# Six edits around the expert blocks and the wide attention of a two-layer decoder kernel: a third PSUM bank, paired transposes, early activation tables, earlier block loads, later roots

## The reference, cut to what matters

```
x = _layernorm(x + _L0_attn_ref(x, ...))          # 16 heads of 8, rope, causal
x = _layernorm(x + _L0_xattn_ref(x, ctx_1024, ..., mask, ...))
x = _layernorm(x + _L0_ffn_ref(x, gate_w, wg, wu, wd))
x = _layernorm(x + _L1_attn_ref(x, W_qkv, W_out)) # 16 heads of 64
x = _layernorm(x + _L1_xattn_ref(x, ctx_1024, ..., mask, ...))
x = _layernorm(x + _L1_ffn_ref(x, W_fc, ln_w, ln_b, W_proj))

# _L0_ffn_ref: 8 experts, 2 per token
top_v, top_i = jax.lax.top_k(x_flat @ gate_w.T, 2)
probs = softmax(top_v)
hidden = jax.nn.silu(x_flat @ wge.T) * (x_flat @ wue.T)
acc + we[:, None] * (hidden @ wde.T)
```

## Time and profile before

| | us |
|---|---|
| median of 3 runs | 412.69 |
| lowest and highest of them | 410.81, 412.75 |
| the profiled execution, its own time | 409.98 |
| its span, first to last instruction | 408.0 |
| PE busy in the span | 347.2 (85%) |
| DVE busy | 252.6 (62%) |
| POOL busy | 186.3 (46%) |
| ACT busy | 183.7 (45%) |

### The profile page before, as it was taken

How to read it: one execution, slowest core, us unless ns; L and a number is a source line. 1 busy time by engine, 2 the same in 40 slices (tenths; PEclk the granted TensorE clock), 3 DMA queues, 4 the chain that set the end, 5 groups by cost and what they waited for, 6 DMA issues and landing times.

```text
span 408.0 us, 9801 instructions
## 1 busy us (share of the span) xinstructions
PE 347.2 (85%) x3718; PEld 263.3 (65%) x3718; DVE 252.6 (62%) x592; ACT 183.7 (45%) x386; POOL 186.3 (46%) x267
## 2 busy tenths in 40 slices
PE   3889899998970899898986874899999989999892
PEld 2556666665870889898975561756667565667572
DVE  1799988896554125732353776435566567887894
ACT  2466676664672422222221251433454335667541
POOL 1767666655455245433227633102222247452673
PEclk9999999996996799999996988699999999999998
DMA  6799900000381011111111100000000000000000
GB/s 199 238 307 300 292 2 2 2 2 28 96 261 39 27 53 40 39 40 53 29 31 42 34 19 2 0 2 2 2 2 2 2 2 2 2 2 2 2 26 26
DMA packets 35938, 22.95 MB, mean 56 GB/s; under 512 B 4142, under 2 KB 33846, under 8 KB 35766
## 3 DMA queue, kind: packets, MB, share of 16 engines
q1 hardware_dynamic: 34582, 19.63, 16.7%
q0 software_dynamic: 1024, 2.10, 1.7%
q10 hardware_dynamic: 288, 0.62, 0.5%
HBM read 14.60 MB, written 7.73 MB: 55 GB/s over the span
## 4 chain that ended last, share of the span: by engine, by line
PE 58%; DVE 14%; issue 8%; POOL 7%; ACT 5%; DMA 5%; SPq 1%; POOLq 0%; DVEq 0%; ACTq 0%
PE banks L426 7%; PE banks L821 6%; PE banks L546 5%; PE banks L523 4%; PE banks L1500 4%; PE banks L1508 4%; PE banks L1531 4%; PE banks L808 4%; DMA XG<-routed_rows 3%; PE banks L852 3%; POOL KB L670 2%; PE banks L530 2%; DVE mx L400 2%; PE banks L495 2%; PE banks L507 2%
## 5 line engine op out<-in xcount | busy, mean ns | idle before, releaser
L330 POOL TENSOR_SCALAR ve<-mv 128x1 f32<-128x1 f32 x40 | 10.6, 265 | 93.8 <-DVE mv L325 93.8
L670 POOL TENSOR_TENSOR KB<-KT,cst 128x512 f32<-128x512 f32 x48 | 49.3, 1047 | 7.5 <-DVE KT L630 5.6
L435 ACT ACTIVATE PT<-banks 128x512 f32<-128x512 f32 x64 | 34.9, 595 | 33.3 <-PE banks L426 32.3
L1523 DVE TENSOR_TENSOR PT<-banks,PR 128x512 f32<-128x512 f32 x23 | 15.9, 691 | 46.6 <-PE banks L1508 40.0
L400 DVE TENSOR_REDUCE mx<-banks 128x16 f32<-128x1024 f32 x32 | 38.7, 1209 | 7.9 <-PE banks L530 5.6
L858 ACT ACTIVATE U<-banks 128x512 f32<-128x512 f32 x40 | 23.9, 597 | 42.5 <-PE banks L821 22.1
L426 PE MATMUL banks<-cst,PR 128*128 128x128 f32 x256 | 36.6, 289 | 6.5 <-POOL PR L887 6.5
L1488 POOL COPY U<-WALL 128x1024 f32 x21 | 21.8, 1040 | 43.8 <-PE banks L1508 42.2
L426 PEld LDWEIGHTS banks<-cst,PR 128*128 128x128 f32 x256 | 29.0, 146 | 10.2 <-POOL PR L887 7.6
L808 PE MATMUL banks<-XT,WQKV 128*128 128x128 f32 x256 | 34.9, 300 | 0.4 <-ACT XT L1703 0.4
L416 ACT ACTIVATE PR<-PR 128x1024 f32<-128x1024 f32 x32 | 33.8, 1057 | 3.1 <-DVE PR L410 2.8
(11 more groups left out here) (181 smaller groups left out, 699.1 us busy)
## 6 DMA issues: line engine op xcount, KB each, us to landing
routed_rows<-zero SPq DMA_DIRECT2D x1, 4544.0 KB, 19.1
U<-in_L_ffn_wg_dram SPq DMA_DIRECT2D x8, 256.0 KB, 5.0
U<-in_L_ffn_wu_dram SPq DMA_DIRECT2D x8, 256.0 KB, 5.3
U<-in_L_ffn_wd_dram SPq DMA_DIRECT2D x8, 256.0 KB, 6.0
U<-in_L_attn_W_qkv_dram SPq DMA_DIRECT2D x1, 1536.0 KB, 22.7
XG<-routed_rows SPq DMA_DIRECT2D x23, 64.0 KB, 1.8
routed_rows<-YS SPq DMA_DIRECT2D x23, 64.0 KB, 1.6
cst<-shape_constants ACTq DMA_DIRECT2D x1, 537.0 KB, 4.6
```

The costliest lines, as they stand in the source:

```text
L435: act.activation(PT[:, n % 2, 4 * m:4 * m + 4, :].rearrange("p r q -> p (r q)"), PS[:, B_PT + m, :], ACT.Copy).then_inc(self.pt.sem, 1)
L670: pool.tensor_tensor(KB[:, n % 2, b], bc(KT[:, n % 2, b, :], 1, 8), bc(cst[:, C_HEAD:C_HEAD + 8], 2, SEQ), ALU.mult).then_inc(self.kb.sem, 1)
```

## The change

1. The wide fills rotate over three banks, `B_K`, `B_Q`, `B_Y`. A fill waits for the copy of the fill three before it.
2. `turn_pe` and `turn_act` take a tuple of tiles: a pair is transposed into two neighbouring quarters of bank 5, and one copy of 256 columns takes both. `TURNED` itself is unchanged.
3. Two one-column activations are added on ACT. A Silu stands between the exponential of the routing weights and the wait for the block map, an Exp at the end of the expert stage. The table loads stand in front of them.
4. On SP six loads stand in front of the first store, and load j+6 in front of store j. There are still four buffers, so that load j still waits for the transpose of block j-4.
5. The roots of tiles 6 and 7 leave `moe.pool`. POOL does them in iteration 3 of its stream, after the shares of tile 0. `extra` is called there twice, with `late` false after the shares and with `late` true at the end, where the scatters of the first stream remain.

```
             def fill(self, pe, f):
-                if f >= 2:
-                    pe.wait_ge(*self.fills_read(f - 2)[self.by(f - 2)])
-                return B_K + f % 2
+                if f >= 3:
+                    pe.wait_ge(*self.fills_read(f - 3)[self.by(f - 3)])
+                return self.bank(f)
+
+            def bank(self, f):
+                return (B_K, B_Q, B_Y)[f % 3]
...
-                for j in range(4):
+                for j in range(6):
                     load(j)
                 for j in range(BLOCKS):
-                    if j + 4 < BLOCKS:
-                        load(j + 4)
+                    if j + 6 < BLOCKS:
+                        load(j + 6)
...
                 act.activation(pk[:, 1, :], pk[:, 0, :], ACT.Exp).then_inc(self.e2.sem, 1)
+                act.activation(warm[:, 0:1], half[:, :], ACT.Silu)
                 act.wait_ge(*self.map.at(8))
...
                 wide.products_copy(act, 0)
-                self.x_act(act, 0)
+                act.activation(warm[:, 1:2], half[:, :], ACT.Exp)
+                self.turn_act(act, (0,))
...
                     if t + 2 < NT:
                         self.gather(pool, t + 2)
-                    self.rsqrt(pool, t)
-                    self.rsqrt(pool, t + 1)
+                        self.rsqrt(pool, t)
+                        self.rsqrt(pool, t + 1)
...
+            def turn_pe(self, pe, ts):
+                norm = self.norm
+                pe.wait_ge(*norm.ln.at(ts[-1] + 1))
+                if ts[0] >= 1:
+                    pe.wait_ge(*norm.xev.at(ts[0]))
+                for k, t in enumerate(ts):
+                    m = pe.transpose(PS[:, B_OX, (2 + k) * P:(3 + k) * P], X[:, t, :], ident)
+                m.then_inc(norm.xmm.sem, len(ts))
+
+            def turn_act(self, act, ts):
+                norm, n = self.norm, len(ts)
+                act.wait_ge(*norm.xmm.at(ts[-1] + 1))
+                act.activation(XT[:, ts[0] * P:(ts[0] + n) * P], PS[:, B_OX, 2 * P:(2 + n) * P], ACT.Copy).then_inc(norm.xev.sem, n)
...
         def post_pe(pe, j, late):
-            for t in TURNED.get((j, late), ()):
-                moe.x_pe(pe, t)
+            if (j, late) in TURNED:
+                moe.turn_pe(pe, TURNED[j, late])
...
-        def no_pool(pool, j):
-            pass
+        def post_pool(pool, j, late):
+            if j == 3 and not late:
+                for t in (NT - 2, NT - 1):
+                    moe.rsqrt(pool, t)
```

More of the change, by code:

```diff
@@ L155, in decoder_kernel @@
         half = sb("half", [P, 1])
+        warm = sb("warm", [P, 2])
         lg = sb("lg", [P, NT, 8])
@@ L868, in qkw_copies @@
                         self.copy(eng, part, QK[:, n % 2, k // 2, 4 * (k % 2):4 * (k % 2) + 4, :].rearrange("p u t -> p (u t)"),
-                                  PS[:, B_K + k % 2, :]).then_inc((self.f_act, self.f_dve)[part].sem, 1)
+                                  PS[:, self.bank(f), :]).then_inc((self.f_act, self.f_dve)[part].sem, 1)
             def vw_copies(self, eng, part, job):
@@ L1247, in stream_pool @@
                     t.stage.shares_pool(pool, t)
+                extra(pool, j, False)
                 b = at(tiles, j - 1)
@@ L1261, in stream_pool @@
                     x.stage.bias_pool(pool, x)
-                extra(pool, j)
+                extra(pool, j, True)
         GROUPS = [(0, 2), (2, 4), (4, 6), (6, 7), (7, 8)]
@@ L1578, in pe @@
                 pe.wait_ge(*fc.bias.at(1))
-                self.x_pe(pe, 0)
+                self.turn_pe(pe, (0,))
             def act(self, act):
@@ L1691, in apply @@
                                   ALU.subtract, ALU.mult).then_inc(norm.ln.sem, 1)
-            def x_pe(self, pe, t):
+            def turn_pe(self, pe, ts):
                 norm = self.norm
-                pe.wait_ge(*norm.ln.at(t + 1))
-                if t >= 1:
-                    pe.wait_ge(*norm.xev.at(t))
-                pe.transpose(PS[:, B_OX, 2 * P:3 * P], X[:, t, :], ident).then_inc(norm.xmm.sem, 1)
-            def x_act(self, act, t):
-                norm = self.norm
-                act.wait_ge(*norm.xmm.at(t + 1))
-                act.activation(XT[:, t * P:(t + 1) * P], PS[:, B_OX, 2 * P:3 * P], ACT.Copy).then_inc(norm.xev.sem, 1)
+                pe.wait_ge(*norm.ln.at(ts[-1] + 1))
[8 more added lines that the diff above has]
+                act.activation(XT[:, ts[0] * P:(ts[0] + n) * P], PS[:, B_OX, 2 * P:(2 + n) * P], ACT.Copy).then_inc(norm.xev.sem, n)
         a0 = Narrow("self0", 0, XT, rope=True, bias=0, row=0, next_row=1)
@@ L1779, in pre_dve, with pre_pool @@
                 moe.place(dve, ROUTED[k])
-        def pre_pool(pool, j):
+        def pre_pool(pool, j, late):
             k = j - DRAIN
-            if k in ROUTED:
+            if late and k in ROUTED:
                 moe.scatter(pool, ROUTED[k])
@@ L1794, in post_act @@
         def post_act(act, j, late):
-            for t in TURNED.get((j, late), ()):
-                moe.x_act(act, t)
+            if (j, late) in TURNED:
+                moe.turn_act(act, TURNED[j, late])
         def post_dve(dve, j, late):
@@ L1885, in _ @@
             moe.pool(pool)
-            stream_pool(pool, post, no_pool)
+            stream_pool(pool, post, post_pool)
         @block.scalar
```

## The result

| | before | changed |
|---|---|---|
| median of 4 runs | 411.75 us (408.19 to 412.75) | 385.56 us (384.45 to 389.23) |
| ratio to before | | 0.9394 (95% interval 0.9304 to 0.9484) |
| profiled execution, its span | 409.98, 408.0 us | 389.23, 387.4 us |
| mean granted clock in it | 0.946 | 0.949 |

The change takes 26.2 us off the median, where 19.9 were forecast. The profiled execution of the changed kernel was the slowest of its four. The other three had spans of 382.5 to 384.7 us.

A forecast was written before the change was run, and what follows sets the result against it. PE, busy 85% of the span, was taken as the bound, through its gaps and half-clock stretches. Blocks 5.0, filling 12.2, steady tiles 1.3 and last tile 1.4 sum to 19.9 us: 412.69 to 392.8 us, range 388.0 to 399.0.

The forecast's parts named there:

- late-landing rival: Expert blocks: slow loads come in bursts that hold the queue, only half of the 5.0 us comes, 395.3 us; chance 0.05.
- The 5.0 us: Expert blocks: gain from earlier loads removing all five PE waits for rows, bounds 4.4 and 5.7 us.
- the Exp's 1.28 us: Filling pipeline: the Exp's table load moves into ACT's wait for the gathers, its 1.28 us counted in the filling's gain.
- My own walk: Filling pipeline: step-by-step timing through tile 1's share transposes, claiming 12.2 us gained, bounds 4.2 and 14.5.
- its next step: Filling, step 2: PE waits 1.8 us for DVE's copy behind tile 1's subtraction, ending its fills at 245.9.
- the rival of the table's hidden drain: Silu table load: an unrecorded 1.4 us drain follows, first block copied 1.0 us late, 393.8 us; chance 0.04.
- The two new waits: Filling: PE's value fills wait for DVE copies, 1.8 us in tile 1 and 0.95 us in tile 2.
- step 3: Filling: POOL's shares of tile 0 are ready by 243.3, before PE asks; their transposes run from 245.9 to 246.8.
- The rival in which DVE takes over: Filling: slower DVE steps leave only POOL's wait and slow restart as gain, 7 instead of 12.2 us, 398; chance 0.08.
- the clock's fall at the new wait: Filling: 1.8 us idle lowers PE's clock for 3 to 6 us, costing 1.5 to 3 us, about 395.0; chance 0.12.
- The slower one: Wide tiles: the clock falls at the new 1.8 us wait and stays low, 424 us; chance 0.03.
- the 0.97 us of a fill: Wide tiles: length of one fill, from three in 3.02 us less the overlap, used in the filling's walk.

The follow-up runs named there:

- no_loads: The changed kernel with block loads back at four ahead instead of six: median 399.11 us, ratio to before 0.9561.
- no_tables: The changed kernel without both early warming activations (Silu and Exp): median 391.69 us, ratio to before 0.9413.
- after_again: The changed kernel itself, run once more on another chip: median 392.52 us, ratio to before 0.9396.
- before_again: The kernel before, unchanged, profiled again in one execution: 415.73 us.
- before_third: The kernel before, unchanged, profiled a third time in one execution: 413.51 us.
- five_ahead: The changed kernel with five block loads in front and load j+5 before store j, instead of six: median 392.55 us, ratio to before 0.9407.
- loads_alone: The kernel before with only the six block loads ahead: median 410.42 us, ratio to before 0.9869.
- roots_alone: The kernel before with only the roots of tiles 6 and 7 moved behind the shares of tile 0: median 407.91 us, ratio to before 0.9802.
- banks_alone: The kernel before with only the third bank for the fills: median 411.91 us, ratio to before 0.9869.
- three_banks_old_wait: The changed kernel with three banks, but each fill waiting for the copy of the fill two before: median 400.78 us, ratio to before 0.9602.

## Why the prediction was right and wrong

**Block loads: right in mechanism, 1.1 us too small.** All five waits went, and no_loads brought the same five back, so they weren't an accident of one execution. The late-landing rival fell. The slow landings themselves stayed (3.4 us for one load of the changed kernel), and the longer lead covered them. The 5.0 us counted the idle time with 0.1 to 0.15 more at each wait; measured against the same blocks of the changed kernel it was 0.18, 5.3 in all. The missing term is the ordinary blocks: 1.2 us over 13 of them, because rows landed just in time there without a recorded wait. I took their 2.85 us as fixed, and it was 2.79 in every kernel with earlier loads and 2.85 again in no_loads. The fourth block took back 0.4 us (3.29 us for 2.85); its length varies from 2.79 to 3.79 over all kernels, so that part is chance. Two blocks of lead weren't needed, one did it.

**Tables: the credit was wrong.** I had the Exp's 1.28 us "leave the path of the filling pipeline". no_tables shows that with the new DVE wait ACT has that much room. My own walk held this, since its next step waits for DVE whatever ACT does, and I did not draw the conclusion. The Silu's load was hidden at both places, as forecast (blocks 68.55 us without the early load, 68.57 with it in after_again). The Trainium skill ("ScalarE: Activation LUTs", What ACT_TABLE_LOAD costs) has a drain behind the load, 2.66 us in all. The trace does not agree at any of the places shown: the next activation starts 0.01 to 0.02 us behind a load of 1.28, and the rival of the table's hidden drain fell with it.

**The filling pipeline: right in mechanism, and as far as the noise allows in size.** The walk gave 12.2 us and the trace 12.9. With before_again or before_third in place of the first profile it would be 13.2 or 11.4, among other things because the clock fell behind the wait of 2.05 or 2.11 us for ACT in the first profile and in before_again, but not in before_third. The two new waits were walked at 1.8 and 0.95 us and measured 1.84 and 0.92, in the places named. POOL's wait went to nothing, as in step 3. The rival in which DVE takes over fell (7 us). So did the clock's fall at the new wait, with a granted clock of 1.00 from 236 to 256 us, and after_again, five_ahead and no_loads have 1.00 behind the same wait. But the reason that I weighed, the wait's length against 2.05 us, does not hold: 2.05 us left the clock up in loads_alone, and 1.83 us was followed by 0.50 in roots_alone. That this rival failed is shown, why it did is not. The slower one, built on the same fall, fell too. Of the 12.9 us, removing the roots costs 6.8, the wait distance 4.0, the pairs 1.4, the table nothing. That makes 12.2, so these four, each taken out by itself, nearly add up, lower clock included. Taken alone they don't: the third bank gives the filling nothing while POOL's wait is there. The 1.1 us that banks_alone lost is lower clock (5.84 us for the query/key fills behind the 2.21 us wait, 4.38 in before).

**Steady tiles: the step that failed.** The sentence was "four tiles lose the wait before the second value fill, 0.19 to 0.24 us idle and 0.3 from start to start: 1.3 us", with 1.4 for the last tile. The stretch gave 4.78 us instead of 2.7: four tiles 3.07 for 1.3, the last tile 1.71 for 1.4. A steady tile went from 12.06 to 11.30 us, by 0.76. The wait that I counted at 0.3 is 0.36 of it. The step had nothing for the rest: 0.17 for the fourth value fill, which waited for DVE's copy without a recorded idle time, 0.10 for the weight loads of these two fills, and 0.11 for the query/key fills. I took the 0.97 us of a fill (0.95 by its starts) as a property of the fill. It contained waiting and weight loads that depend on how early the wait is met, and the merged row of matmuls shows neither. three_banks_old_wait shows the cause, since it takes back all of it with the wait's distance alone. The same sits in the filling.

**What is left.** The trace shows 23.8 us in the edited stretches, and the medians 26.2 (by the interval 21.2 to 28.7, since 411.75 times 0.9304 and 0.9484 leave these) and 25.2 on the other chip (23.7 to 26.7 by the same working). So the forecast's error of 6.3 us against the measured difference is 3.9 in named terms, 1.1 (blocks), 0.7 (filling) and 2.1 (steady tiles), and 2.4 that lie within the spread of the unedited stretches (133.0 to 140.7 us before the first block over all profiles). Nothing shown here assigns them to the change. The range was too narrow for another reason: its low end, the profiled execution less 22 us, added the upper bounds of some terms only, and had nothing for a term missing altogether, which the steady tiles and the ordinary blocks had.

## What to carry to other kernels

With two buffers, or with loads issued just in time, a wait can be met late where the profile shows no idle time, and it then holds back the next group's weight loads too. Before you take the length of a matmul group as fixed, compare its starts with the end of the copy or landing that it waits for, read the weight loads' row, and try a wait one step further back. Where several stalls stand in a row in a filling pipeline, walk engine by engine and credit only the one that comes last: the third bank was worth nothing there alone and 4 us together with the others, while a table load taken off an engine that isn't last gained nothing. Compare executions stretch by stretch and look at a stretch that nobody edited first, since here it varied by more than some of the parts are worth.

## What the runs showed of the hardware

- The same fill of 4 fp32 matmul instructions (128x512) took 0.91 us from start to start with its weight loads in one group behind a late wait (before and three_banks_old_wait, second fill of a steady tile) and 0.86 us with them under the fill before it (changed kernel).
- In before, a block's transpose started 0.04 us behind the landing of its rows at 11 of the last 18 blocks, and six of these transposes have no idle time of PE in front of them.
- The length of a wait alone did not tell whether the granted clock fell. Behind 1.84 us it stayed at 1.00 (changed kernel) and behind 1.83 us it fell to 0.50 within 2 us (roots_alone). Behind 2.05 us it was 0.50 in before and 1.00 in loads_alone. Behind 2.59 and 2.60 us, and behind every wait of 6.03 us, it was 0.50.
- A wait of 1.9 to 3.3 us on "another core or an unknown queue" stands between 98 and 114 us in the chain of 11 of the 16 profiled executions, of a program on one core, and not in the others, whichever kernel it is.
- The stretch behind tile 7, not edited in any kernel, took 71.2 to 71.3 us everywhere but in loads_alone (72.42) and no_loads (73.9). Both have a lower granted clock there, 0.72 over 6 us and 0.68 and 0.75 over 12 us, where before_again has 1.00. Why it fell is open.
